# Attention values of a float32 two-layer kernel: high parts, ones and low parts in one stationary tile, two passes a chunk, the last low column by GpSimd or a pass of its own

## The reference

```
scores = jnp.einsum('bhqd,bhkd->bhqk', q, k) * scale
attn = jax.nn.softmax(scores, axis=-1)
out = jnp.einsum('bhqk,bhkd->bhqd', attn, v)
```

## Time and profile before

| What | Value |
|---|---|
| median of 3 runs | 4304.78 us (4302.63 to 4305.23) |
| the profiled execution | 4291.18 us, its span 4289.1 us |
| mean granted clock of PE in it | 0.949 |
| PE busy, of the span | 3884.6 us, 91% |
| DVE busy | 3610.1 us, 84% |
| ACT busy | 2635.9 us, 61% |
| POOL busy | 2219.0 us, 52% |
| the attention's slots, in the span | about 930 to 3790 us |

### The profile page before, as it was taken

How to read it: one execution, slowest core, us unless ns; L and a number is a source line. 1 busy time by engine, 2 the same in 40 slices (tenths; PEclk the granted TensorE clock), 3 DMA queues, 4 the chain that set the end, 5 groups by cost and what they waited for, 6 DMA issues and landing times. The chain is left out here.

```text
span 4289.1 us, 54983 instructions
## 1 busy us (share of the span) xinstructions
PE 3884.6 (91%) x17786; PEld 2959.5 (69%) x17786; DVE 3610.1 (84%) x4517; ACT 2635.9 (61%) x3523; POOL 2219.0 (52%) x1837
## 2 busy tenths in 40 slices
PE   7959978759999999999999999999999999989563
PEld 4635536538888888888888888888888888867321
DVE  7845549859999999999999999999999999946511
ACT  6624334337777777777777777777777777732221
POOL 2547757825555555555555555555555555520164
PEclk9969989969999999999999999999999999989776
DMA  7224447842233222332223322223222232056286
GB/s 270 55 53 65 67 118 247 283 85 56 50 69 67 56 56 50 66 71 55 57 50 63 75 52 61 51 61 76 52 59 51 57 79 52 15 160 220 86 240 163
DMA packets 335313, 388.12 MB, mean 90 GB/s; under 512 B 141516, under 2 KB 263185, under 8 KB 322483
## 3 DMA queue, kind: packets, MB, share of 16 engines
q1 hardware_dynamic: 310966, 358.28, 32.7%
q0 software_dynamic: 24064, 26.32, 3.6%
HBM read 236.66 MB, written 117.79 MB: 83 GB/s over the span
## 5 line engine op out<-in xcount | busy, mean ns | idle before, releaser
L1561 POOL TENSOR_TENSOR at_pl<-at_pf,at_ph 128x512 fp32r<-128x512 f32 x1024 | 1330.6, 1299 | 1341.1 <-ACT at_ph L1708 1340.8
L1707 ACT ACTIVATE at_pf<-at_ps_s 128x1024 f32<-128x1024 f32 x1024 | 1051.2, 1027 | 745.7 <-PE at_ps_s L1757 745.7
L1624 DVE TENSOR_TENSOR at_pl<-at_pf,at_ph 128x512 fp32r<-128x512 f32 x1024 | 1355.4, 1324 | 20.6 <-ACT at_ph L1708 20.6
L1606 DVE TENSOR_REDUCE at_mx<-at_ps_u 128x2 f32<-128x1024 f32 x1024 | 1249.8, 1220 | 22.5 <-PE at_ps_u L1741 22.4
L1708 ACT ACTIVATE at_ph<-at_ps_s 128x1024 fp32r<-128x1024 f32 x1024 | 1043.1, 1019 | 0.0
L1757 PE MATMUL at_ps_s<-at_q,at_k 66*128 66x512 f32 x2048 | 819.7, 400 | 0.0
L1756 PE MATMUL at_ps_s<-at_q,at_k 128*128 128x512 f32 x2048 | 811.4, 396 | 0.5 <-ACT at_ph L1708 0.5
L1773 PE MATMUL at_ps_v<-at_ph,at_vh 128*128 128x512 f32 x2048 | 809.2, 395 | 0.2 <-POOL at_pl L1561 0.2
L1775 PE MATMUL at_ps_v<-at_pl,at_vh 128*128 128x512 f32 x2048 | 809.1, 395 | 0.0
L1774 PE MATMUL at_ps_v<-at_ph,at_vl 128*128 128x512 f32 x2048 | 808.1, 395 | 0.0
L1741 PE MATMUL at_ps_u<-at_k,at_qp 128*128 128x512 f32 x2048 | 647.5, 397 | 64.2 <-DMA at_q<-at_low 48.4
(11 more groups left out here) (261 smaller groups left out, 4034.2 us busy)
## 6 DMA issues: line engine op xcount, KB each, us to landing
at_k<-kT SPq DMA_DIRECT2D x64, 512.0 KB, 10.1
at_q<-qT SPq DMA_DIRECT2D x64, 512.0 KB, 9.2
wgu<-Wgu_in SPq DMA_DIRECT2D x64, 384.0 KB, 5.2
qT<-pj_rot SPq DMA_DIRECT2D x32, 512.0 KB, 5.2
vT<-pj_vo SPq DMA_DIRECT2D x16, 1024.0 KB, 5.7
kT<-pj_rot SPq DMA_DIRECT2D x32, 512.0 KB, 3.2
at_raw<-qT SPq DMA_DIRECT2D x32, 512.0 KB, 4.8
at_raw<-kT SPq DMA_DIRECT2D x32, 512.0 KB, 6.7
```

Of the source, the lines that this page charges most:

```text
L1561: pool.tensor_tensor(pl[:, n % NP, at], pf[:, n % NP, at], ph[:, n % NP, at].bitcast(F32), ALU.subtract).then_inc(s["pl2_ready"], 1)
L1606: dve.tensor_reduce(mx[:, qb % 2, 2 * i:2 * i + 2], ps_u[:], X, ALU.max).then_inc(s["u_max"], 1)
L1624: dve.tensor_tensor(pl[:, n % NP, at], pf[:, n % NP, at], ph[:, n % NP, at].bitcast(F32), ALU.subtract)\
L1707: act.activation(pf[:, n % NP], ps_s[:, n % 2], ACT.Exp, scale=DH ** -0.5)
```

## The change

The stationary tile `va` of a chunk has 128 columns: 64 high parts of the values, one column of ones, and the low parts of 63 of the 64 values (all but the first). One matmul with `ph` then gives high by high, the denominator, and low by high for 63 columns; a second with `pl` gives the rest (and low by low). The low part of the first value's column (`vl0`) gets its product in one of two ways:

- for the odd chunks (`own_product`), by a third matmul with a tile `vx` that holds that one column and zeros;
- for the even chunks, by POOL: `ph` times `vl0` (one number a partition), added up over the block's eight even chunks in `acc` (`first_sums`), the last sum in fp32r in `accr`; one matmul a block (`fold`, with `first`, ones in one column) adds it over the partitions into `ps_v`.

Because the high and low results now lie in different partitions of `ps_v`, ACT copies twice a block (`o_all`, and `o_lo` from partitions 64 to 127, the denominator's row scaled to zero), and POOL adds the two (`whole`).

POOL has no time for its half of `pl` then, so DVE makes all 1024 columns, and reads the float32 exponentials from PSUM: ACT writes `ph` first, then the second exponential in place over `ps_s`. `scores(n + 2)` must therefore wait for DVE's `low_part(n)` (`pl_ready`). The subtraction of the keys' and queries' low parts (`take_low`) goes from DVE to POOL. Semaphore steps called `turns` on POOL fall away. In the linear attention at the start of the kernel, SP's loads of the expert biases (`load_bias`) come one step later, and DVE's last `factors` one step earlier.

```
             NP = 4
+        NX = PER
+        SUMS = 2 * PER - NX
+        TAIL = 4
...
+            def own_product(c):
+                x = (c - (KC - 2 * NX + 1)) // 2
+                return x if c % 2 == 1 and x >= 0 else None
...
             def _(pool):
...
-                def low_part(g, n):
-                    pool.wait_ge(s["p_ready"], g * SLOTS + (n + 3))
-                    stand_alone(pool, s["turns"])
-                    at = slice(QB, 2 * QB)
-                    pool.tensor_tensor(pl[:, n % NP, at], pf[:, n % NP, at], ph[:, n % NP, at].bitcast(F32),
-                                       ALU.subtract).then_inc(s["pl2_ready"], 1)
...
+                def first_sums(g, hh, n):
...
+                    pool.wait_ge(s["p_ready"], g * SLOTS + (n + 1))
+                    for j in range(2):
+                        c = 2 * c2 + j
+                        if own_product(c) is not None:
+                            continue
...
+                        if done > 0:
+                            pool.wait_ge(s["sums"], TAIL + done)
+                        if c == 0:
+                            pool.tensor_scalar(acc[:], p, low0, None, ALU.mult).then_inc(s["sums"], 1)
+                            continue
+                        scaled += 1
+                        pool.tensor_scalar(part[:, scaled % 2], p, low0, None, ALU.mult).then_inc(s["scaled"], 1)
+                        pool.wait_ge(s["scaled"], scaled)
...
+                        pool.tensor_tensor(to, acc[:], part[:, scaled % 2], ALU.add).then_inc(s["sums"], 1)
+
+                def whole(g, qb):
+
+                    pool.wait_ge(s["o_ready"], 4 + 2 * (g * NQB + qb + 1))
+                    pool.tensor_tensor(o_st[:, qb % 2], o_lo[:, qb % 2], o_all[0:DH, qb % 2], ALU.add).then_inc(s["o_added"], 1)
...
                     for n in range(SLOTS):
-                        if n + 1 < SLOTS or prepare:
-                            low_part(g, n + 1)
+                        first_sums(g, hh, n)
+                        if n % PER == 3 and g * NQB + n // PER > 0:
+                            whole((g * NQB + n // PER - 1) // NQB, (n // PER - 1) % NQB)
+                        if not prepare:
+                            continue
+                        i = n - 8
+                        if 0 <= i < 2 * NQB and i % 2 == 0:
+                            take_low(nxt, 1 - hh, i // 2)
...
             def _(dve):
...
                 def low_part(g, n):
-                    dve.wait_ge(s["p_ready"], g * SLOTS + (n + 3))
-                    at = slice(0, QB)
-                    dve.tensor_tensor(pl[:, n % NP, at], pf[:, n % NP, at], ph[:, n % NP, at].bitcast(F32), ALU.subtract)\
+                    dve.wait_ge(s["p_ready"], g * SLOTS + (n + 1))
+                    dve.wait_ge(s["pf_ready"], g * SLOTS + (n + 1))
+                    if n >= NP or not isinstance(g, int) or g > 0:
+                        dve.wait_ge(s["pv_done"], g * SLOTS + (n + 1))
+                    dve.tensor_tensor(pl[:, n % NP], ps_s[:, n % 2], ph[:, n % NP].bitcast(F32), ALU.subtract)\
                         .then_inc(s["pl_ready"], 1)
...
-                        if cutting:
-                            take_low(nxt, 1 - hh, i // 2)
...
             def _(act):
...
-                        act.activation(pf[:, n % NP], ps_s[:, n % 2], ACT.Exp, scale=DH ** -0.5)
+                        act.wait_ge(s["sums"], TAIL + pr * (2 * NQB * SUMS) + sums_before(n - NP + 1))
                         act.activation(ph[:, n % NP], ps_s[:, n % 2], ACT.Exp, scale=DH ** -0.5)\
                             .then_inc(s["p_ready"], 1)
+                        act.wait_ge(s["p_ready"], pr * (2 * SLOTS) + (n + 1))
+                        act.activation(ps_s[:, n % 2], ps_s[:, n % 2], ACT.Exp, scale=DH ** -0.5)\
+                            .then_inc(s["pf_ready"], 1)
...
             def _(pe):
...
                     if j == 0:
-                        pe.wait_ge(s["p_ready"], g * SLOTS + (n + 1))
+                        if g > 0 or n > 1:
+                            pe.wait_ge(s["pl_ready"], g * SLOTS + (n - 1))
...
-                    pe.matmul(out, vh[:, hh, c], ph[:, n % NP, keys], start=c == 0, stop=False)
-                    pe.matmul(out, vl[:, hh, c], ph[:, n % NP, keys], start=False, stop=False)
-                    m = pe.matmul(out, vh[:, hh, c], pl[:, n % NP, keys], start=False, stop=c == KC - 1)
+                    pe.matmul(out, va[:, hh, c], ph[:, n % NP, keys], start=c == 0, stop=False)
+                    m = pe.matmul(out, va[:, hh, c], pl[:, n % NP, keys], start=False, stop=False)
+                    if own_product(c) is not None:
+                        m = pe.matmul(out, vx[:, hh, own_product(c)], ph[:, n % NP, keys], start=False, stop=False)
                     if j == 1:
                         m.then_inc(s["pv_done"], 1)
+
+                def fold(block_):
+
+                    pe.wait_ge(s["sums"], TAIL + (block_ + 1) * SUMS)
+                    pe.matmul(ps_v[:, block_ % 2], first[:], accr[:, block_ % 2], start=False, stop=True).then_inc(s["fold_done"], 1)
...
                         values(g, hh, n, 0)
+                        if n % PER == 0 and g * NQB + n // PER > 0:
+                            fold(g * NQB + n // PER - 1)
```

More of the change, by code:

```diff
@@ L538, in _ @@
                     j = i - 8
+                    if i == NT:
+                        factors(Q - 1, mv2, std2, rstd2, nb2, "2")
                     if i == FIRST:
@@ L571, in _ @@
                     t = i - 2
[L572 removed]
+                    if tile(t) and t % 4 == 3 and t < NT - 1:
                         factors(t // 4, mv2, std2, rstd2, nb2, "2")
@@ L1409, in softmax_attention @@
             vf = sb("vf", [P, 2, KC, DH])
-            vh = sb("vh", [P, 2, KC, P], F32R)
-            vl = sb("vl", [P, 2, KC, P], F32R)
+            va = sb("va", [P, 2, KC, P], F32R)
+            vx = sb("vx", [P, 2, NX, P], F32R)
+            vl0 = sb("vl0", [P, 2, KC])
+            acc = sb("acc", [P, QB])
+            part = sb("part", [P, 2, QB])
+            accr = sb("accr", [P, 2, QB], F32R)
+            first = sb("first", [P, P], F32R)
+            others = sb("others", [P, 1])
             mx = sb("mx", [P, 2, 2 * PER])
@@ L1431, in softmax_attention, with sums_before @@
             block = ctx.enter_context(nc.Block())
+            def own_product(c):
+                x = (c - (KC - 2 * NX + 1)) // 2
+                return x if c % 2 == 1 and x >= 0 else None
+            def sums_before(n):
+                return n // PER * SUMS + sum(own_product(c) is None for c in range(2 * (n % PER)))
             @block.sync
@@ new lines, in own_products, with take_low @@
+                def own_products(g, hh):
+                    pool.wait_ge(s["vl0_ready"], g + 1)
+                    pool.tensor_copy(vx[:, hh, :, 0:1], vl0[:, hh, KC - 2 * NX + 1::2].unsqueeze(2)).then_inc(s["vx_ready"], 1)
+                def take_low(base, hh, i):
+                    pool.wait_ge(s["cut_ready"], base * NQB + (i + 1))
+                    pool.wait_ge(s[f"low{i % 2}"], base * 64 + 32 * (i // 2))
+                    pool.tensor_tensor(low[:, i % 2], raw[hh][:, i * QB:(i + 1) * QB].bitcast(F32),
+                                       cut[:, i % 2].bitcast(F32), ALU.subtract).then_inc(s["low_ready"], 1)
@@ L1584, in _ @@
                 head(PAIRS - 1, 1, False)
+                whole(HEADS - 1, NQB - 1)
             @block.vector
@@ L1724, in _ @@
             def _(pe):
-                pe.wait_ge(s["fixed"], 4)
+                pe.wait_ge(s["fixed"], 7)
                 def products(base, hh, half, j):
@@ L1802, in _ @@
                 head(PAIRS - 1, 1, False)
+                fold(HEADS * NQB - 1)
     def output_projection(self):
```

88 lines of the change are left out of this document (58 added, 30 removed).

## The result

The changed kernel takes 4812.76 us (median of 4 runs, 4807.0 to 4814.61) where the one before takes 4304.74 in the same comparison: a ratio of 1.1175, 95% interval [1.116, 1.119]. That is 508 us slower. The forecast had the sign, but not the case: it said 4337 and a range up to 4430.

What follows compares the result with a forecast made beforehand. PE was taken as the bound: 83.1 + 6.9 + .6 = 90.6 us a head instead of 89.6, +30 over 31 heads, tail +3, so 4291.2 becomes 4324; with 13.6 for the median, 4337 us, range 4150 to 4430.

Steps and rivals of the forecast that it cites:

- PE's own work: Attention matmuls: 11 a slot and one more a block, 83.1 us a head instead of 89.6.
- The subtraction from PSUM: DVE's 1024-column low-part subtraction in the attention loop: about 1.2 us, not held by POOL.
- case (d): Rival, 3%: POOL holds DVE's subtraction after all, DVE needs 2.9 us a slot; 4450 or more.
- I take .70, near twice the cast less a fixed part: POOL's 128x512 scaling: .70 us, between .40 and 1.29, giving POOL 79 us a head, under PE's 83.1.
- case (c): Rival, 12%: POOL's scaling costs as much as a two-input pass, 98 us a head, POOL becomes the bound; 4575.
- The stabilisers: Once a block `nmh` and `nml` wait for POOL, 1.65 us; PE loses 1.7, 6.9 a head; likeliest case, 54%.
- .63 us to spare: Loop from scores of slot n to slot n+2: T + 4.50 against 5.13 for PE's own pace.
- T + 2.07: Start of DVE's maxima in a slot, T being PE's start of that slot; .44 behind its seventh matmul.
- The cut: DVE's cut instruction in the attention: meets a busy POOL, some .45 us more on average; .6 a head.
- The clock: PE's clock in the attention: stays at 1.00 despite stalls of 1.7 in 22 us; a small risk.
- The start: Linear attention at the kernel's start: the edits there change 0, and 2 us either way at most.
- the tail: End of the last block: a sum, `fold`, two copies and `whole` where one copy was; +3 us.

Runs made afterwards that it cites:

- scale_copy_stab: Changed kernel with POOL's scaling as a plain copy, `nmh` from a second reduction and `nml` made behind the next subtraction: 4141.42 us, ratio 0.964.
- scale_copy: Changed kernel with POOL's scaling as a plain copy, the multiplication left out: 4297.8 us, ratio 1.0009 to the kernel before.
- after_stab: Changed kernel with only the stabilisers changed (`nmh` from a second reduction, `nml` made behind the next subtraction): 4816.49 us, ratio 1.1184 to the kernel before.
- no_sums: Changed kernel with POOL's scalings and sums left out except in the first two blocks, semaphores still counted: 4176.51 us, ratio 0.9722.
- bcast8_stab: Changed kernel, eight chunks on POOL, scaling as a two-input broadcast product, `nmh` from a second reduction, `nml` behind the next subtraction: 4269.65 us, ratio 0.9914.
- la_only: Kernel before with only the change's edits to the linear attention part: 4302.89 us, ratio 0.9995.
- scale_bcast: Changed kernel with POOL's scaling as a two-input product, the number a partition broadcast over the columns: 4409.98 us, ratio 1.0272.

## Why the prediction was wrong

**PE's own work, right.** Eleven matmuls a slot and one fold a block, 83.1 us a head; with a cheap scaling and the stabilisers moved, the attention ran at 84.5 (scale_copy_stab).

**The subtraction from PSUM, right.** It was taken as 1.2 and not held by POOL. It took 1219 ns on average beside a POOL that was 95% busy, so case (d) did not come.

**The step that failed: "I take .70, near twice the cast less a fixed part."** The scaling took 1.57, and POOL, held to be free, became the bound: 105.2 us a head against its 79. The bounds failed too: "from above: the two-input pass, 1.29" rested on one input being no dearer than two, which is false for this instruction; only the lower end, which the copy's .61 confirms, held. The forecast's own sum with this one term put right gives 79 + 32 x (1.57 - .70) = 106.8 us a head for POOL, and (106.8 - 89.6) x 31 + 3 + 4304.8 = 4841, against 4813 measured. So case (c), given 12%, was what happened: its sign, PE waiting in `fold`, came, and its formula was .6% off; the price in it was too small, which left its own 4575 too low as well. (c) said that POOL passes PE at .82 us, near the middle between .40 and 1.29. That alone should have given it more than 12%.

**The stabilisers, right in kind and in neither size.** This was the likeliest case, and in the changed kernel it is covered by POOL's pace: scale_copy and after_stab show both halves of that. Where the scaling is cheap, the forecast of 4337 (33 over before) met 4297.8 (4 over). A head lost 89.5 - 83.1 = 6.4 us, where 6.9 + .6 had been said. Where it was lost shows in the length of the slot behind the stabilisers (n % 8 == 3, from its first score matmul to the next slot's, mean of 1500 to 3500 us; the slots with n % 8 of 1 and 5 take 2.56 to 2.57 in all three runs, as forecast for a plain one):

| Forecast | scale_copy | no_sums | scale_copy_stab |
|---|---|---|---|
| 2.57 + 1.71 = 4.28 | 3.79 | 2.97 | 2.63 |

This slot makes 4 x 1.22 = 4.9 of the 6.4. The parts are not those of the sum. "1.65 us of waits" were (368 - 171) + (846 - 162) = 881 ns, half of it. But the ".63 us to spare" was overstated: with nothing held, in no_sums, the slot is still .40 late, where the sum had .06. The forecast let the maxima start at T + 2.07; they start at T + 2.4, because DVE is at the subtraction before until then, and the subtraction behind the stabilisers starts at T + 4.24 instead of T + 3.93. Two errors partly cancelled, and that the total came near is luck. The other 1.5 us a head (.6 was said) lie in other slots. The cut took 807 ns against 419 beside an idle POOL (no_sums), .39 more where .45 was said; how much of the 1.5 that makes is open, as are the .7 us that no_sums loses outside the slot above.

The Trainium skill (SBUF — State Buffer, section Who interferes with whom) says that a reduction on DVE never meets GpSimd at the shared port; the traces agree (159 ns for `nmh` as a reduction against 368 as a multiplication).

**What was not seen at all: SP's queue.** The prediction named `whole` as work for POOL, but not the store that waits for it, nor the rows queued behind the store. PE waited 90 us of 2500 there. It does not set the time, since POOL has no gap to give back: in after_stab it is 130 us of 2000, and the time is the same. With a cheaper scaling it goes away by itself (1.8 us of 2000 in bcast8_stab).

**The clock.** It was called a small risk. With the gaps PE's granted clock fell to 0.94 in the attention, from 1.00; a matmul's share of PE's busy time is 1721.88 / 6766 = 254 ns instead of 233, of which the gaps make a part too, since the last matmul ahead of a gap counts in full. As POOL waits for nobody, this cost nothing here. With the stalls that the forecast had in mind (scale_copy) the clock stayed at 1.00, as it said.

**The start, right; the tail, too small.** The linear attention part makes no difference (la_only). From the last scores to the end the changed kernel takes 517 us where the one before takes 505, +12 for the +3 of the sum: POOL is behind with its sums, so the last `fold` starts 12.3 us behind the last scores, in scale_copy 5.1. There the tail is +1.

## What to carry to other kernels

Moving work to an idle engine needs the price of the very instruction there, and a row of another instruction of the same shape is not a bound: measure one before building on it. Count the receiving engine's whole loop and write down at which price it becomes the bound; if that price lies between your bounds, the case is an even one and not a tail. Here a chunk's extra product costs .233 us on PE and 1.57 + 1.29 on POOL, so the split has to be set by POOL's idle time, and a small instruction that it holds up should be moved off the path or into a form that isn't held. Moved off the path, the held instruction can still delay the one behind it.

## What the runs showed of the hardware

- On GpSimd, 128x512 in float32: a copy 611 ns, a multiplication of two operands with one broadcast along the columns 1039, a sum of two full operands 1289, and `tensor_scalar` with one multiplication 1492 with a constant and 1570 with a number a partition. The dearest of the four has one tensor input. The spread is small (1552 to 1747 ns over 896 of them at 1570), so it is not a few held ones that make the mean.
- On DVE beside a busy POOL: `tensor_reduce` of 16 numbers a partition is not held (158 to 170 ns on average in each run), nor is a subtraction with one input in PSUM (1216 to 1219 ns); four numbers a partition by `tensor_scalar`, `scalar_tensor_tensor` or `tensor_tensor` are: about .16 us unheld, they took up to 1.87 (scale_bcast). A single-input copy on POOL holds them as a sum does: in scale_copy `nml` ends with the copy, at 2511.27 and 2511.25.
- ACT's exponential of 128x1024 takes 1008 ns from PSUM to PSUM (in float32) and 1025 from PSUM to SBUF (in fp32r).
